# Raw maxima turned at full width and split afterwards; row DMAs on one queue; stacks loaded per group

## The reference

```python
xn = _layernorm(x)
s = attention(xn)      # 32 heads of 16, 8 key/value heads, RoPE, causal softmax
g = _silu(moe(xn))     # 8 experts, top 2, relu, mean of the two
x = x + s * g
xn = _layernorm(x)
s = long_convolution(xn)   # S4 kernel from a 512-point transform
g = _silu(xn @ w_deq.T + bias)
x = x + s * g
```

## Time and profile before

| | |
|---|---|
| timed runs, median (lowest to highest) | 665.72 us (664.77 to 666.27), 3 runs |
| profiled execution, span from first to last instruction | 663.2 us; the page gives no other time of its own, the median lies 2.5 us above this span |
| TensorE busy | 627.2 us, 95%, mean granted clock 0.987 |
| VectorE busy | 552.0 us, 83% |
| ScalarE busy | 287.0 us, 43% |
| GpSimd busy | 238.2 us, 36% |
| SyncE's DMA queue | 68098 packets, 86.90 MB, 53.5% of 16 engines' span |
| ScalarE's DMA queue | 5038 packets, 6.84 MB, 4.2% |

### The profile page before, as it was taken

The page is one execution under the profiler, slowest core; times in us unless marked ns, Lnnn a source line. Parts: engine busy times, 40 slices in busy tenths (PEclk is TensorE's granted clock), DMA queues, the critical chain, the costliest instruction groups (busy, mean ns, idle before and its releaser), DMA issues.

```text
span 663.2 us, 12226 instructions
## 1 busy us (share of the span) xinstructions
PE 627.2 (95%) x3565; PEld 338.9 (51%) x3565; DVE 552.0 (83%) x1788; ACT 287.0 (43%) x535; POOL 238.2 (36%) x364
## 2 busy tenths in 40 slices
PE   8999999998999999999999999999999999789997
PEld 5788784433433334433443344443444343478886
DVE  6698999869978888989888798897789975689994
ACT  4353325434434435444444444443455443444441
POOL 3777641333323212332221322322222115576620
PEclk9999999969989999999999999999999999899999
DMA  7599989889788564675954649667276527768842
GB/s 262 141 336 266 337 239 173 146 164 273 152 268 161 166 139 80 154 132 188 194 105 98 136 109 220 125 173 152 52 167 111 171 72 241 156 145 217 217 104 79
DMA packets 79902, 113.10 MB, mean 171 GB/s; under 512 B 9704, under 2 KB 42664, under 8 KB 79840
## 3 DMA queue, kind: packets, MB, share of 16 engines
q1 hardware_dynamic: 68098, 86.90, 53.5%
q0 software_dynamic: 6704, 18.62, 11.8%
q10 hardware_dynamic: 5038, 6.84, 4.2%
HBM read 72.15 MB, written 39.65 MB: 169 GB/s over the span
## 4 chain that ended last, share of the span: by engine, by line
PE 55%; DVE 25%; DMA 8%; issue 4%; SPq 3%; POOL 2%; ACT 1%; ACTq 0%; DVEq 0%; POOLq 0%
PE bank L1672 13%; DVE bank L1390 12%; PE bank L1023 8%; PE bank L1591 7%; PE bank L2162 6%; PE bank L1644 5%; PE bank L1683 4%; PE bank L2167 4%; DMA w_e<-expert_rows,slots 3%; PE bank L1617 3%; DVE arena L1390 2%; DMA qt<-arena 2%; DMA qt<-turned_parts 2%; DVE m_parts L1403 2%; DVE m_parts L1405 1%
## 5 line engine op out<-in xcount | busy, mean ns | idle before, releaser
L1390 DVE CUSTOM_DVE_ANT_0 bank<-bank,cst 128x384 f32<-128x384 f32 (+3 forms) x512 | 234.9, 521 | 47.6 <-PE bank L1591 44.5
L1514 ACT ACTIVATE arena<-bank 128x512 f32<-128x512 f32 x320 | 170.9, 599 | 180.2 <-PE bank L1617 149.7
L1332 POOL TENSOR_SCALAR_AFFINE_SELECT arena<-arena 128x512 f32<-128x512 f32 x128 | 80.7, 643 | 309.2 <-ACT arena L1514 309.2
L1672 PE MATMUL bank<-w_e,arena 128*128 x312 | 162.2, 626 | 0.0
L1591 PE MATMUL bank<-kt,qt 48*128 48x512 f32 (+1 forms) x496 | 111.0, 338 | 5.6 <-DVE arena L1390 5.0
L1591 PEld LDWEIGHTS bank<-kt,qt 48*128 48x128 f32 x496 | 70.1, 187 | 83.9 <-DVE arena L1390 51.7
L1617 PE MATMUL bank<-qt,kt 50*128 50x512 f32 x256 | 88.2, 452 | 2.4 <-DMA qt<-arena 2.0
L1644 PE MATMUL bank<-arena 128*32 128x512 f32 (+3 forms) x1024 | 84.8, 445 | 0.4 <-ACT arena L1514 0.4
L1672 PEld LDWEIGHTS bank<-w_e,arena 128*128 128x128 f32 x312 | 54.6, 193 | 58.0 <-issue 54.3
L1390 DVE DVE_READ_ACCUMULATOR2_ANT arena<- 128x1 f32 x512 | 71.9, 140 | 0.0
L1683 PE MATMUL bank<-w_proj,arena 128*128 128x512 f32 x128 | 67.6, 636 | 0.0
(11 more groups left out here) (167 smaller groups left out, 942.7 us busy)
## 6 DMA issues: line engine op xcount, KB each, us to landing
qt<-turned_parts SPq DMA_DIRECT2D x96, 128.0 KB, 4.7
turned_parts<-qk_parts SPq DMA_DIRECT2D x8, 1280.0 KB, 7.2
gathered_rows<-s_tok SPq DMA_DIRECT2D x39, 256.0 KB, 5.3
arena<-gathered_rows SPq DMA_DIRECT2D x39, 256.0 KB, 3.4
expert_rows<-arena SPq DMA_DIRECT2D x39, 256.0 KB, 4.5
w_e<-in_L_ffn_W_e ACTq DMA_DIRECT2D x24, 256.0 KB, 6.2
kt<-turned_parts SPq DMA_DIRECT2D x96, 64.0 KB, 4.4
arena<-in_L_attn_x SPq DMA_DIRECT2D x16, 256.0 KB, 6.1
```

What stands on the lines that cost most here:

```text
L1332: g.affine_select(out=diag, in_=diag, compare_op=ALU.is_ge, fill=0.0, base=0, pattern=[[0, 2], [0, HALF], [1, P]], channel_multiplier=-1). ...
L1390: i = v.tensor_tensor_reduce(out=part, in0=part, in1=const("mask")[:, S - w:], scale=1.0, scalar=LOWEST, op0=ALU.add, op1=ALU.max, accum_o ...
L1514: nc.scalar.activation(pt[:, s, first:second + 1:second - first].rearrange("p c r q -> p c (r q)"), s2_bank(b, h, n).rearrange("p (c x) -> ...
L1672: i = t.matmul(bank[7], xgt[:, m % 2, k * P:(k + 1) * P], w_e[:, ex[m], k, :], start=False, stop=(k == KB - 1))
```

## The change

`maxima_parts` becomes `maxima_columns`: one copy puts the raw maxima twice into a tile `m_cols` of 2 x 8 x 8 = 128 columns (the rest zero from the start). The transpose takes all 128 columns. `maxima_rows` then makes the high part of all 128 rows, waits for it, and subtracts it in those rows whose constant `less` is -1 (the second copies); the other rows are rounded only. The rows are not negated, so the two extra rows of `kt` are -1.0. Both row DMAs are issued by SyncE. `load_stack` loads one group with 8 DMAs instead of two groups with 12, four groups ahead, in every group; where the two parts lie under each other in the stack, one DMA brings both to 32 partitions. The semaphores of the stacks are four instead of two, and the arena grows by 200 words.

```diff
-            buf = h // 2 % 2
-            q_rows = qk_d[b][:, R * HD * h:R * HD * (h + 2), :].rearrange("c (g s i r) t -> c s i g (r t)", g=2, s=2, r=HALF)
-            k_rows = qk_d[b][:, D + HD * h:D + HD * (h + 2), :].rearrange("c (g i) t -> c i g t", g=2)
+            keys, queries, loaded = kt[:, h // 2 % 2, h % 2], qt[:, h // 2 % 2, h % 2], b_ld[h % 4]
+            k_rows = qk_d[b][:, D + HD * h:D + HD * (h + 1), :]
+            q_rows = qk_d[b][:, R * HD * h:R * HD * (h + 1), :].rearrange("c (s i r) t -> s c i (r t)", s=2, r=HALF)
             for s in range(2):
-                for piece, (of_q, of_k) in enumerate(((0, 0), (0, 1), (1, 0))):
-                    at = 64 * s + HD * piece
-                    if (b, h) != (0, 0):
-                        e.dma_start(kt[at:at + HD, buf].bitcast(F32), k_rows[of_k]).then_inc(b_ld[buf], 16)
-                    e.dma_start(qt[at:at + HD, buf].bitcast(F32).rearrange("i g r t -> i g (r t)"), q_rows[of_q, s]).then_inc(b_ld[buf], 16)
+                at = 64 * s
+                if b or h > 1:
+                    e.dma_start(keys[at:at + 2 * HD].bitcast(F32), k_rows).then_inc(loaded, 16)
+                    e.dma_start(keys[at + 2 * HD:at + ROWS].bitcast(F32), k_rows[0]).then_inc(loaded, 16)
+                e.dma_start(queries[at:at + HD].bitcast(F32).rearrange("i r t -> i (r t)"), q_rows[s, 0]).then_inc(loaded, 16)
+                e.dma_start(queries[at + HD:at + ROWS].bitcast(F32).rearrange("i r t -> i (r t)"), q_rows[s]).then_inc(loaded, 16)
...
-            if due(at := nth_of(NJ, b, h, -2 * NJ)):
+            if due(at := nth_of(NJ, b, h, -3 * NJ)):
...
-            v.tensor_scalar(m_parts[:, :, 0], rows, -1.0, None, ALU.mult).then_inc(dve_steps, st.one())
-            e.wait_ge(dve_steps, st.count())
-            v.scalar_tensor_tensor(out=m_parts[:, :, 1], in0=rows, scalar=-1.0, in1=m_parts[:, :, 0].bitcast(F32),
-                                   op0=ALU.mult, op1=ALU.subtract).then_inc(b_mx, 1)
+            nc.vector.tensor_copy(m_cols[:, :, 0:2], rows.unsqueeze(2).to_broadcast([P, 2, 2, HALF * TPB])).then_inc(b_mx, 1)
...
-            nc.vector.tensor_copy(m_rows, S1_BANK[nth_of(NJ, b, h, NJ + 2) % 3][0:2 * 2 * HALF * TPB, 0:P]).then_inc(b_me, 1)
+            v.tensor_copy(m_high[:, :], turned_at(b, h)).then_inc(dve_steps, st.one())
+            e.wait_ge(dve_steps, st.count())
+            v.scalar_tensor_tensor(out=m_rows[:, :], in0=m_high[:, :].bitcast(F32), scalar=const("less"), in1=turned_at(b, h),
+                                   op0=ALU.mult, op1=ALU.add).then_inc(b_me, 1)
...
+            t.transpose(turned_at(b, h), m_cols.rearrange("p s c x -> p (s c x)"), ident).then_inc(b_tm, 1)
...
@@ act_b: go
-                    if b * NG + h + 1 < NB * NG:
-                        maximum_rows(e, *next_group(b, h, 1), 1)
@@ sp_b: go
                     if b * NG + h + 1 < NB * NG:
-                        maximum_rows(e, *next_group(b, h, 1), 0)
-                    if h % 2 and b * NG + h + 3 < NB * NG:
-                        load_stacks(e, *next_group(b, h, 3))
+                        for s in range(2):
+                            maximum_rows(e, *next_group(b, h, 1), s)
+                    if b * NG + h + 4 < NB * NG:
+                        load_stack(e, *next_group(b, h, 4))
```

More of the change, by code:

```diff
@@ L121 @@
 for _name, _n in (("ident", P), ("half", 1), ("eps", 1), ("minus", 1), ("mask", S), ("tri", P), ("cos", TPB * 8), ("sin", TPB * 8), ("s4", 16),
-                  ("lower", E * E), ("i128", NT), ("i128m", MT + 1), ("tile", MT), ("iota", P), ("tilenum", TOPK * NT), ("part", 1), ("sel", E)):
+                  ("lower", E * E), ("i128", NT), ("i128m", MT + 1), ("tile", MT), ("iota", P), ("tilenum", TOPK * NT), ("part", 1), ("sel", E), ("less", 1)):
     COLS[_name] = (_at, _at + _n)
@@ L156, in constants @@
     put("minus", -1.0)
+    put("less", -1.0 * (p // 8 % 8 == 1))
     put("sel", np.arange(E)[None, :] == p[:, None] % 32)
@@ L460, in sp_a @@
                         load_first(e)
-            load_stacks(e, 0, 0)
+            for h in (0, 1):
+                load_stack(e, 0, h)
         def dve_a(e, st):
@@ L466, in dve_a @@
             v.memset(be3[:, :], 0.0).then_inc(dve_steps, st.one())
+            v.memset(m_cols, 0.0).then_inc(dve_steps, st.one())
             e.wait_ge(a_load, 16)
@@ L622, in dve_a @@
                 maxima(e, 0, 1, n)
-            maxima_parts(e, st, 0, 1)
-            maxima_rows(e, 0, 1)
+            maxima_columns(e, 0, 1)
+            maxima_rows(e, st, 0, 1)
             dve_experts(e, st)
@@ L1207, in build @@
         row_max = take([P, R, TPB])
-        m_parts = parts("m_parts", [P, 2, 2, HALF * TPB], "arena", used[0])
-        take([P, 2, 2, HALF * TPB])
-        m_rows = take([P, P])[0:2 * 2 * HALF * TPB]
+        m_cols = take([P, 2, 8, HALF * TPB])
+        m_high = parts("m_high", [P, P], "arena", used[0])
+        take([P, P])
+        m_rows = parts("m_rows", [P, P], "arena", used[0])
+        take([P, P])
         rsum = take([P, QB])
@@ L1230, in build @@
         b_first = sem("b_first")
-        b_ld = sems("b_ld", 2)
+        b_ld = sems("b_ld", 4)
         b_wo = sem("b_wo")
@@ L1371, in build, with first_half, turned_at @@
         LOWEST = -3.0e38
-        def first_half(n):
+        def first_half(b, h, n):
             return (n + 1) % 2, n // 2
+        def turned_at(b, h):
+            return S1_BANK[nth_of(NJ, b, h, NJ + 2) % 3][:, 0:P]
         def maxima(e, b, h, n):
             v = nc.vector
-            s, kind = first_half(n)
+            s, kind = first_half(b, h, n)
             if n == 0 and due(at := nth_of(1, b, h, 0)):
@@ L1627, in turn_maxima @@
             e.wait_ge(b_mx, nth_of(1, b, h, 1))
-            t.transpose(S1_BANK[nth_of(NJ, b, h, NJ + 2) % 3][0:2 * 2 * HALF * TPB, 0:P], m_parts.rearrange("p s c x -> p (s c x)").bitcast(F32), ident)\
-                .then_inc(b_tm, 1)
+            t.transpose(turned_at(b, h), m_cols.rearrange("p s c x -> p (s c x)"), ident).then_inc(b_tm, 1)
         def values(e, b, h, j):
@@ L1819, in sp_b @@
                 load_expert(e, x)
-            load_stacks(e, 0, 2)
+            for h in (2, 3):
+                load_stack(e, 0, h)
             for b in range(NB):
```

34 lines of the change are left out of this document (15 added, 19 removed).

## The result

| | median (lowest to highest) | ratio to before, 95% interval |
|---|---|---|
| before | 665.25 us (664.28 to 666.27) | |
| changed kernel | 713.06 us (709.1 to 715.48) | 1.0714 [1.0667, 1.0762] |

The forecast was 678.4 us, range 659 to 708. The direction was right, the time lies above the range. The profiled execution of the changed kernel has a span of 713.7 us.

The account below looks back on a forecast made before the run. TensorE and VectorE were taken to bound the loop alternately, waiting for each other. Terms of -4.9 and +17.6 us gave +12.7 on the 663.2 us span, 675.9, plus 2.5 to the median: 678.4 us, range 659 to 708.

Parts of the forecast that it names:

- the sum of the stacks: Attention loop: four large stack loads per group run on two of 16 engines, tiles behind them land late: +17.6 us.
- Where: Loop: twelve of 39 tiles each 1.1 us late, +13 us; groups 2 to 8, with more traffic, +4.6.
- Landing: A tile issued behind the stacks at T+6.1 lands at T+14.3, T being the start of the maxima's transpose; due T+13.2.
- Rival (c): Stack loads saturate the two engines, so row DMAs come late in every group: 707 us or more; chance 10%.
- Sum without the stacks: Maxima columns, weight load, rows and row DMAs of the loop and first stage together: -4.9 us.
- Columns: Before each turn one copy replaces two dependent instructions, cutting TensorE's idle before the transpose: -7.5 us, bounds 0 and -11.1.
- full-width weight load: At the turn, TensorE's wider weight load takes 0.05 us more in 14 groups where the columns come last: +0.6 us.
- rival (d): Stacks spread over the engines, but the copy of the maxima always ends with the last select: 664.7 us; chance 4%.
- Per-group loads: SyncE waits and issues eight stack loads in every group; by itself harmless, the stacks having 13 us more time.
- ScalarE's relief: In each group ScalarE no longer spends 0.62 us on a row DMA's issue and a wait; least busy, so nothing.
- Rival (a): The four large stack loads spread over 16 engines after all, leaving a sum of -4.9: 660.8 us; chance 14%.

Follow-up runs that it names:

- m1: Kernel without computation, loading 128 KB to 32 partitions in three forms: eight in a row take 22.6 us (outermost size 2), 9.0 (two DMAs), 6.8 (one source of 32 rows).
- e2: Changed kernel with each of a group's four two-part loads issued as two DMAs to 16 partitions: 660.84 us, ratio 0.9916 to the kernel before.
- e12: Changed kernel with the stacks issued behind the tiles of place 1 instead of ahead of them: 696.38 us, ratio 1.0472 to the kernel before.
- e8: Changed kernel, two-part stack loads included, with both row DMAs issued by ScalarE on its own queue: 732.55 us, ratio 1.0996 to the kernel before.
- e11: Changed kernel with only the first four stacks in the two-part form, all later loads as DMAs of 16 partitions: 676.80 us, ratio 1.0155 to the kernel before.
- e4: Kernel before with only the new maxima (columns, full-width turn, rows), old stack loads, row DMA of `s` = 1 still on ScalarE: 668.38 us, ratio 1.0046.
- e5: Kernel before with the new maxima and both row DMAs issued by SyncE, but the old stack loads: 669.26 us, ratio 1.0067.
- e9: Kernel before with only the loads changed: one stack per group, 12 DMAs of 16 partitions, four groups ahead: 664.84 us, ratio 1.0002.
- e6: Changed kernel with all two-part loads split into DMAs of 16 partitions and the row DMA of `s` = 1 back on ScalarE: 662.82 us, ratio 0.9954 to before.
- e7: Changed kernel with the two-part loads of the queries split, only the two of the keys left in two-part form: 657.72 us, ratio 0.9909 to the kernel before.

## Why the prediction was wrong

**The step that failed is the sum of the stacks, +17.6 us, by its size.** Its mechanism (a load with outermost size 2 on two engines, tiles and rows standing behind it) is shown by m1, e2 and e12; e8 fits it. The measured value is 52.2 us (713.06 less e2's 660.84). Within the sum, the start stood at nothing, and every one of twelve tiles at the same 1.1 us. From the starts of the turns, changed kernel less e2:

| stretch | changed, e2 | measured | predicted |
|---|---|---|---|
| turns 0 to 2 | 52.9, 36.5 us | +16.4 | nothing |
| turns 2 to 9 | 122.8, 109.6 us | +13.2 | +4.6 |
| turns 9 to 31 | 314.2, 291.2 us | +22.9 | +13 |

These are one execution each; their spans differ by 54.6 us, of which 2.5 lie behind the last turn.

- *The start* was not priced. The stacks of the first two groups, with 512 KB of two-part queries, are issued from 95.4 us on. The last goes out at 101.06 and takes 16.84 us in the chain of waits, while TensorE is ready for group 1 from 107.6 us (117.93 less 10.31):

```profile
101.06 16.84 DMA qt<-turned_parts
```

  e11 has the term of the first four stacks alone: 676.80 less 660.84, 16 us.
- *Where* it is late was wrong. I priced twelve tiles at 1.1 us each. Of the 22 times between turns from turn 9 on, sixteen are within 0.4 us of e2's, and those from turns 13, 21, 23 and 28 are 7.0, 3.8, 4.2 and 5.0 us longer. In the first two a tile is late (by 4.4 and 3.6 us) and with it the rows, in the other two only the rows of the maxima (2.4 and 3.2). An average load of the two engines says whether a queue forms on the average, not what the worst group pays.
- *Landing*: forecast T+14.3 (its 0.4 us for the receipt stands in no row). In the group of turn 317.28 the tile landed at 334.63, T+17.4. It was issued at T+7.0 rather than T+6.1, because the list ahead of it had two rows at 0.65 and four loads at 0.61 to 0.63 instead of 0.47 us, and then took 10.32 us instead of 8.2.
- *The clock* was not priced at all. These are the four worst groups, first in the changed kernel, then in e2:

```profile
330.28:350.10 19.82, 16.18 (x77) 7.14 (x78) 12.17 (x43) 6.42 (x12) 3.39 (x6) 0.83 0.41 125
445.50:462.97 17.47, 14.86 (x77) 6.31 (x78) 13.04 (x50) 6.41 (x12) 3.39 (x6) 0.90 0.47 148
477.46:494.62 17.16, 14.89 (x76) 6.21 (x78) 12.17 (x44) 6.33 (x12) 2.00 (x4) 0.90 0.41 133
547.85:565.42 17.57, 14.20 (x74) 5.58 (x75) 11.56 (x48) 6.20 (x12) 3.45 (x5) 0.90 0.45 140
```

```profile
301.07:313.89 12.82, 12.66 (x77) 5.74 (x78) 11.96 (x43) 6.30 (x12) 3.39 (x6) 1.00 0.54 154
407.40:421.09 13.69, 13.14 (x77) 5.80 (x78) 13.03 (x51) 6.52 (x12) 3.40 (x6) 1.00 0.70 220
434.65:447.57 12.92, 12.76 (x76) 5.71 (x77) 12.06 (x44) 6.12 (x12) 2.00 (x4) 1.00 0.41 119
500.82:513.35 12.53, 12.06 (x73) 5.25 (x74) 11.45 (x48) 6.09 (x12) 3.45 (x5) 1.00 0.48 135
```

They last 20.1 us longer (72.02 less 51.96). TensorE is busy 60.12 us instead of 50.62 for the same work (304 and 303 product records): 9.5 us of the 20.1 are longer busy time at the lower granted clock, 10.6 are idle. In these groups each microsecond that TensorE stood went with nearly one more of slower work.

Rival (c) came nearest: it had rows late in every group and 707 us or more. The time fits it, the mechanism only in part, since most groups were not late.

**Sum without the stacks, -4.9 us.** e2, which is that sum's kernel but for four more issues per group, is at -4.8. Its terms did not come out as worked, though. In the profiled executions e2 is 7.7 us shorter than before from turn 9 to 31 (291.2 and 299.0), but 3.3 us longer from turn 2 to 9 (109.6 and 106.3).

- *Columns, -7.5.* TensorE's idle time before the turn fell from 11.1 us to 2.5 in e2, as forecast. In e2's timeline of turn 18 it is gone:

```profile
367.46 1.02 PE L1677 MATMUL bank<-w_e,arena 128*128 x2 [0.16 <-issue]
...
367.77 0.27 DVE L1411 COPY arena<-arena 128x32 f32<-128x32 f32 x1
368.10 0.14 PEld L1634 LDWEIGHTS bank<-cst,arena 128*128 128x128 f32 x1 [0.45 <-DVE arena L1411]
368.32 0.27 PE L1634 MATMUL bank<-cst,arena 128*128 128x128 f32 x1
```

  The columns are there at 368.04, while TensorE works at expert products until 368.48 by this row (ends of products are modelled), and the turn follows without idle time. Where TensorE still stands (0.31 to 0.32 us in turns 3, 7, 11, 15, 19, 23, 27 and 29), the product starts 0.06 us after the copy, the same as after L1405 (448.20 to 448.26 in the earlier trace rows). So the 0.05 us for the full-width weight load, +0.6 in the sum, show nowhere.
- *The copy* is held up by the selects in those eight turns (0.56 to 0.58 us; in turn 19 it ends at 381.48, the selects at 381.45). In the other 22 from turn 2 on it takes 0.18 to 0.34 us, so rival (d), which had it held always, is out.
- *Per-group loads* were costed only as harmless. They are what lets the columns pay at all: with the old loads the maxima lose 2.7 us (e4) or 3.4 (e5), with the new ones they gain 4.0 (660.84 less e9's 664.84). The resource without slack is the arrival of a pair of stacks, for which the waits of before showed 0.7 us in 2 places.
- *ScalarE's relief, "so nothing"*, was wrong in the groups. With one row on ScalarE (e4, e6) TensorE's idle time before the turn is gone as well (3.0 and 2.5 us left), yet the undisturbed groups stay as long as before; taking the row away makes them 0.30 to 0.33 us shorter, which is about all that they gain. The medians of e6 and e2 differ by 2.0 us with overlapping intervals, so the size in the time stays open. Whether moving the issue alone, without the columns, would gain was not tried; before, ScalarE waits for L1413 only once, 3.5 us. With both rows on ScalarE (e8) a group is 1.0 to 1.7 us longer. The Trainium skill (Trainium Kernel Development and Optimization, Key Constraints) has the issue from several engines as a saving of issue time only; e4, e6 and e8 show that it can also cost, where the engine waits for the row's data ahead of work that others need.

Rival (a), 660.8, and e2, 660.84, agree; part of that is luck, since the groups behind turn 9 gained more than the whole sum and the ones before it lost.

What stays open: whether e7 is really faster than e2 (657.72 and 660.84, intervals that overlap, taken in different comparisons; from turn 9 to 31 their profiles agree within 0.2 us), and why single groups of the first batch differ by some microseconds between kernels that differ in little (from turn 2 to 3: 18.1 us before, 16.8 in e4, 19.4 in e2; from turn 6 to 7: 13.6, 13.6, 19.3).

## What to carry to other kernels

Merging two DMAs into one with an outermost size of 2 saves an issue and can take fourteen of sixteen engines away; look at the small packets of a DMA that exists, and measure the new form alone before building on it. A queue on shared engines costs where something urgent is issued behind it, so list what is issued after the large transfers, with due times, group by group and at the start, rather than comparing averages. Before speeding up a step, check which resource is just in time for the old pace (here the pair of stacks): its wait is near zero in the profile of before, and it is the next bound.

## What the hardware showed that I had not expected

- A stall of TensorE was followed by half its clock in the worst group: 1.32 us of work in 4.6 us, then a granted clock of 0.50 for 3.4 us and 0.58 for 4 more. Four expert products take 3.62 us there and 1.98 us later in the same group.
- A DMA with an outermost size of 2 holds its issuer longer: 0.61 to 0.63 us on SyncE, against 0.42 for one of 16 partitions (two rows of a group on ScalarE: 1.3 us).
- Behind 393 KB on two engines, transfers over all sixteen land two to three times as late (10.3 to 10.8 us for 256 KB, where the page of before has 3.4 to 5.3), although the 16 engines move only 42 to 58 GB/s at first. A second queue did not help: in e8 a row DMA on ScalarE's queue took 6.09 us. That the two queues meet at the same two engines fits this and was not shown by itself.
